# A four-layer decoder on one core: the second layer's attention and projection bias moved into matrix products, and the feed-forward's sums one block later

## The reference

```python
x = x + _L0_ffn_ref(_layernorm(x), router_w, router_b, expert_w, expert_b)   # one of 8 experts for each token
x = x + _L1_attn_ref(_layernorm(x), Wqkv, bqkv, Wproj, bproj)
x = x + _L1_xattn_ref(...)
x = x + _L1_ffn_ref(_layernorm(x), w_gate, w_up, w_down)
```

## Time and profile before

| what | value |
|---|---|
| median of 3 runs | 6096.39 us (6095.18 to 6096.58) |
| the profiled execution | 6100.48 us, of it the span 6098.6 us |
| TensorE busy | 5427.2 us, 89% of the span, granted clock 0.936 in the mean |
| VectorE busy | 3993.1 us, 65% |
| ScalarE busy | 2848.8 us, 47% |
| GpSimd busy | 1761.1 us, 29% |
| loads and stores | 125.10 MB |
| second layer's attention, first product to last output | 1713.89 to 1793.46 us |
| its projection, first turn to the last product | 1793.71 to 1814.58 us |
| second layer's feed-forward, first up to last down product | 2061.05 to 2144.16 us |

### The profile page before, as it was taken

One profiled execution on the slowest core, in us unless ns is written; L12 is line 12 of the kernel. 1 busy time (PEld: TensorE's weight loads), 2 busy tenths in 40 slices (PEclk: granted clock), 3 DMA queues, 4 the chain that ended last, 5 costly groups with the idle time before them and its releaser, 6 DMA issues.

```text
span 6098.6 us, 76361 instructions
## 1 busy us (share of the span) xinstructions
PE 5427.2 (89%) x29994; PEld 2957.3 (48%) x29994; DVE 3993.1 (65%) x6951; ACT 2848.8 (47%) x4524; POOL 1761.1 (29%) x1903
## 2 busy tenths in 40 slices
PE   7987999999977879999998989997958879799978
PEld 4443454454444645555555653336834444333355
DVE  5666767767676579888886257763267744788632
ACT  4553444444115466656564236672135555366600
POOL 3211333333024036454464022203422122222021
PEclk9997999999989989998999889998979989899989
DMA  1000000000000000000000000004410000000033
GB/s 53 1 3 1 1 1 1 1 1 1 21 30 1 8 28 1 1 1 1 1 1 1 10 1 1 1 1 155 166 35 1 1 17 1 32 1 1 32 101 106
DMA packets 39364, 125.10 MB, mean 21 GB/s; under 512 B 5588, under 2 KB 20940, under 8 KB 32990
## 3 DMA queue, kind: packets, MB, share of 16 engines
q1 hardware_dynamic: 28206, 67.70, 3.2%
q0 software_dynamic: 10800, 52.52, 2.5%
HBM read 99.42 MB, written 24.90 MB: 20 GB/s over the span
## 4 chain that ended last, share of the span: by engine, by line


## 5 line engine op out<-in xcount | busy, mean ns | idle before, releaser
L74 PE MATMUL PS<-SC 128*128 128x128 f32 (+14 forms) x14896 | 2814.3, 428 | 163.7 <-ACT SC L80 56.1
L80 ACT ACTIVATE SC<-PS 128x1024 f32<-128x1024 f32 (+7 forms) x2555 | 1933.7, 782 | 1892.6 <-PE PS L74 1560.7
L74 PEld LDWEIGHTS PS<-SC 128*128 128x128 f32 (+6 forms) x14896 | 1214.4, 129 | 1502.6 <-issue 603.7
L95 DVE TENSOR_REDUCE SC<-PS 128x1 f32<-128x512 f32 (+5 forms) x2368 | 1516.6, 680 | 603.0 <-PE PS L74 590.2
L83 POOL TENSOR_TENSOR SC<-SC 128x1024 f32<-128x1024 f32 (+3 forms) x892 | 1190.0, 1344 | 1490.0 <-ACT SC L80 1245.7
L74 PE MATMUL PS<-AR 128*128 128x128 bf16 (+6 forms) x4000 | 1121.6, 393 | 64.2 <-DVE SC L83 16.2
L74 PEld LDWEIGHTS PS<-AR 128*128 128x128 f32 (+2 forms) x4000 | 599.5, 174 | 461.3 <-issue 269.5
L77 PE MATMUL PS<-AR,SC 128*104 128x128 bf16 (+3 forms) x4664 | 518.4, 254 | 322.4 <-DVE SC L86 156.3
L74 PE MATMUL PS<-SC,AR 128*128 128x512 f32 (+7 forms) x1938 | 760.4, 516 | 46.1 <-POOL SC L83 12.8
L77 PEld LDWEIGHTS PS<-AR,SC 128*104 128x104 bf16 (+3 forms) x4664 | 402.1, 135 | 537.6 <-DVE SC L86 142.3
L80 ACT ACTIVATE SC<-SC 128x512 f32<-128x512 f32 (+7 forms) x870 | 445.1, 563 | 454.0 <-DVE SC L86 217.0
(11 more groups left out here) (82 smaller groups left out, 2165.3 us busy)
## 6 DMA issues: line engine op xcount, KB each, us to landing
SC<-in_pk11e SPq DMA_DIRECT2D x8, 1152.0 KB, 5.9
SC<-in_pk11e SPq DMA_DIRECT2D x8, 1028.0 KB, 5.1
xg<-SC SPq DMA_DIRECT2D x16, 512.0 KB, 6.8
SC<-yg SPq DMA_DIRECT2D x16, 512.0 KB, 7.6
yg<-AR SPq DMA_DIRECT2D x8, 512.0 KB, 5.8
AR<-in_pk SPq DMA_DIRECT2D x2, 1562.0 KB, 8.0
AR<-in_pk SPq DMA_DIRECT2D x2, 1538.0 KB, 12.9
AR<-in_pk SPq DMA_DIRECT2D x6, 512.0 KB, 4.9
```

Source lines behind the costliest of these rows:

```text
L74: return Step(self.real and self.real.matmul(*a, **k))
L80: return Step(self.real and self.real.activation(*a, **k))
L95: return Step(self.real and self.real.tensor_reduce(*a, **k))
```

## The change

1. **Bias of the attention as a product.** A new class `Parts` holds the bias row of 1024 values split into three bf16 parts, in partitions 0, 32 and 64 of a tile `bias` that is zero elsewhere, and a bf16 tile of ones, `oneb`. TensorE adds `oneb[0:65].T @ bias[0:65]` to each of the attention's banks (four products a tile) as the last of the accumulation, and to the projection's (`Project` gets an argument `bias`; one product for each of 16 tiles). `AddBias` of stage 3 goes.
2. **Where the parts are made.** The load of `pk3r` moves from stage 3 to the `sp` of `TopOne`, behind `pk2e`; VectorE makes the parts in three pieces after the token tiles i = 1, 2 and 4 of `TopOne`.
3. **PSUM read by ScalarE.** The four reads of a tile's banks are now copies on ScalarE (`out(i)`), with no addition; ScalarE's order is out(0), out(1), exp(0), out(2), exp(1) and so on. `out(i)` waits for the value products of tile i - 2 on VectorE and GpSimd. TensorE waits for ScalarE's copies in place of VectorE's additions.
4. **Feed-forward.** VectorE's loop calls `summed(k - 2)` at f = 1 and `root(k - 2)` at f = 3 of block k, and the sums of blocks 2 and 3 come behind the loop.

```diff
 class Project(Stage):
-                                     start=c == 0, stop=c == 1)
+                                     start=c == 0, stop=c == 1 and self.bias is None)
+                    if self.bias is not None:
+                        t = e.matmul(K.PS[:, 4 + 2 * (k % 2) + g, 256 * z:256 * z + 256], *self.bias, start=False, stop=True)
...
 class TopOne(Stage):
         e.dma_start(self.eb, self.K.ins["pk2e"]).then_inc(self.eb_ready, "all")
+        self.K.parts.sp(e)
...
+            if i in (1, 2, 4):
+                K.parts.dve(e, (1, 2, 4).index(i))
...
+class Parts:
+    def __init__(self, K):
+        heap = Heap(K.view, TOT - 3200, TOT)
+        self.K, self.ready = K, K.load("d_pk3r")
+        self.rows, self.rest = heap.take([1024]), heap.take([1024])
+        self.bias, self.part, self.oneb = heap.take([1024], BF16), heap.take([1024], BF16), heap.take([128], BF16)
+
+    def sp(self, e):
+        e.dma_start(self.rows, self.K.ins["pk3r"]).then_inc(self.ready, "all")
+
+    def dve(self, e, step):
+        vv, bias, part, rest, rows = self.K.vv, self.bias, self.part, self.rest, self.rows
+        if step == 0:
+            e.memset(self.oneb, 1.0).then_inc(vv, "3 one")
+            e.memset(bias, 0.0).then_inc(vv, "3 zero")
+            e.wait_ge(self.ready, "all")
+            e.tensor_copy(part[0:65, :], rows[0:65, :]).then_inc(vv, ("3 part", 0))
+            e.wait_ge(vv, "3 zero")
+            e.tensor_copy(bias[0:1, :], rows[0:1, :]).then_inc(vv, ("3 bias", 0))
+        elif step == 1:
+            e.wait_ge(vv, ("3 part", 0))
+            e.tensor_tensor(rest[0:65, :], rows[0:65, :], part[0:65, :], ALU.subtract).then_inc(vv, ("3 rest", 0))
+            e.wait_ge(vv, ("3 rest", 0))
+            e.tensor_copy(part[0:65, :], rest[0:65, :]).then_inc(vv, ("3 part", 1))
+        else:
+            e.tensor_copy(bias[32:33, :], rest[32:33, :]).then_inc(vv, ("3 bias", 1))
+            e.wait_ge(vv, ("3 part", 1))
+            e.tensor_tensor(rest[64:65, :], rest[64:65, :], part[64:65, :], ALU.subtract).then_inc(vv, ("3 rest", 1))
+            e.wait_ge(vv, ("3 rest", 1))
+            e.tensor_copy(bias[64:65, :], rest[64:65, :]).then_inc(vv, ("3 bias", 2))
...
 class BatchAttention(Stage):   # pe
-                        e.wait_ge(K.vv, ("3 qkv", i - 2, b, z))
+                        e.wait_ge(K.av, ("3 qkv", i - 2, b, z))
...
+                    e.wait_ge(K.vv, ("3 bias", 2))
+                    e.matmul(PS[:, bank, 0:hi - lo], self.oneb[0:65, :], self.bias[0:65, lo:hi], start=False, stop=True).then_inc(K.mm, ("3 qkv", i, b, z))
...
+        def out(i):            # act
+            x = i % 2
+            if i >= 2:
+                e.wait_ge(K.vv, ("3 pv", i - 2, 1))
+                e.wait_ge(K.gv, ("3 pv", i - 2, 1))
+            for b in range(2):
+                for z in range(2):
+                    lo, hi = (0, 512) if z == 0 else (512, 768)
+                    e.wait_ge(K.mm, ("3 qkv", i, b, z))
+                    e.activation(self.qk[x][:, b, lo:hi], K.PS[:, 4 * x + 2 * b + z, 0:hi - lo], ACT.Copy).then_inc(K.av, ("3 qkv", i, b, z))
+        out(0)
         for i in range(8):
-            e.wait_ge(self.K.vv, ("3 s-max", i))
+            if i + 1 < 8:
+                out(i + 1)
+            e.wait_ge(K.vv, ("3 s-max", i))
...
-            for b in range(2):  # dve
-                for z in range(2):
-                    lo, hi = (0, 512) if z == 0 else (512, 768)
-                    e.wait_ge(K.mm, ("3 qkv", i, b, z))
-                    e.tensor_tensor(qk[:, b, lo:hi], PS[:, 4 * x + 2 * b + z, 0:hi - lo], self.rows[:, lo:hi], ALU.add).then_inc(vv, ("3 qkv", i, b, z))
...
-    return [norm, Meet(K, "n3"), AddBias(K, "bias3", K.X, st.rows[:, 768:1024], st.rows_ready), st,
-            Meet(K, "a3"), K.tail]
+    return [norm, Meet(K, "n3"), st, Meet(K, "a3"), K.tail]
...
 class Swiglu(Stage):           # dve
-            if k > 0 and f == 3:
-                summed(k - 1)
-                if self.next is not None:
-                    self.next.root(e, 0, k - 1)
+            if k > 1 and f == 1:
+                summed(k - 2)
+            if k > 1 and f == 3 and self.next is not None:
+                self.next.root(e, 0, k - 2)
         low(4 * nf - 1)
         if self.next is not None:
-            for k in range(3):
+            for k in range(2):
                 self.next.scale(e, 0, k)
-        summed(3)
-        if self.next is not None:
-            self.next.root(e, 0, 3)
-            self.next.scale(e, 0, 3)
+        for k in (2, 3):
+            summed(k)
+            if self.next is not None:
+                self.next.root(e, 0, k)
+                self.next.scale(e, 0, k)
```

More of the change, by code:

```diff
@@ L422, with __init__ @@
     next = None
-    def __init__(self, K, tag, O, wo, dst):
-        self.K, self.tag, self.O, self.wo, self.dst = K, tag, O, wo, dst
+    def __init__(self, K, tag, O, wo, dst, bias=None):
+        self.K, self.tag, self.O, self.wo, self.dst, self.bias = K, tag, O, wo, dst, bias
         self.done = (K.mm, (tag, "o", 3, 1))
@@ L1340, in __init__ @@
         self.norm = EarlyLogits(K, "n2", [layer(K.X, take([NT, D]))], self)
+        K.parts = Parts(K)
     def bank(self, n):
@@ L1507, in __init__ @@
         take = K.scr.take
-        self.rows = take([1024])
-        self.rows_ready = K.load("d_pk3r")
+        self.bias, self.oneb = K.parts.bias, K.parts.oneb
         self.qk = [take([2, 768]) for _ in range(2)]
@@ L1515, in __init__ @@
         self.O = take([NT, D])
-    def sp(self, e):
-        e.dma_start(self.rows, self.K.ins["pk3r"]).then_inc(self.rows_ready, "all")
     def pe(self, e):
@@ L1528, in pe @@
                     if i >= 2:
-                        e.wait_ge(K.vv, ("3 qkv", i - 2, b, z))
+                        e.wait_ge(K.av, ("3 qkv", i - 2, b, z))
                     for c in range(2):
-                        t = e.matmul(PS[:, bank, 0:hi - lo], K.XNT[:, c, b * S + 128 * i:b * S + 128 * i + 128], self.wqkv[:, c, lo:hi],
-                                     start=c == 0, stop=c == 1)
-                    t.then_inc(K.mm, ("3 qkv", i, b, z))
+                        e.matmul(PS[:, bank, 0:hi - lo], K.XNT[:, c, b * S + 128 * i:b * S + 128 * i + 128], self.wqkv[:, c, lo:hi],
+                                 start=c == 0, stop=False)
+                    e.wait_ge(K.vv, ("3 bias", 2))
+                    e.matmul(PS[:, bank, 0:hi - lo], self.oneb[0:65, :], self.bias[0:65, lo:hi], start=False, stop=True).then_inc(K.mm, ("3 qkv", i, b, z))
     def act(self, e):
+        K = self.K
+        def out(i):
[9 more added lines that the diff above has]
+        out(0)
         for i in range(8):
-            e.wait_ge(self.K.vv, ("3 s-max", i))
-            e.activation(self.ex[i % 2], self.sc[i % 2], ACT.Exp, scale=0.25).then_inc(self.K.av, ("3 exp", i))
+            if i + 1 < 8:
+                out(i + 1)
+            e.wait_ge(K.vv, ("3 s-max", i))
+            e.activation(self.ex[i % 2], self.sc[i % 2], ACT.Exp, scale=0.25).then_inc(K.av, ("3 exp", i))
     def dve(self, e):
-        K, PS, vv = self.K, self.K.PS, self.K.vv
-        e.wait_ge(self.rows_ready, "all")
+        K, vv = self.K, self.K.vv
         for i in range(8):
@@ L1547, in dve @@
                 e.wait_ge(K.gv, ("3 pv", i - 2, 1))
-            for b in range(2):
-                for z in range(2):
-                    lo, hi = (0, 512) if z == 0 else (512, 768)
-                    e.wait_ge(K.mm, ("3 qkv", i, b, z))
-                    e.tensor_tensor(qk[:, b, lo:hi], PS[:, 4 * x + 2 * b + z, 0:hi - lo], self.rows[:, lo:hi], ALU.add).then_inc(vv, ("3 qkv", i, b, z))
             Q, Kk, V = qk[:, :, 0:256], qk[:, :, 256:512], qk[:, :, 512:768]
-            e.wait_ge(vv, ("3 qkv", i, 1, 1))
+            e.wait_ge(K.av, ("3 qkv", i, 1, 1))
             for r in range(2):
@@ L1591, in stages_3 @@
     norm = follow(K, Norm(K, "n3", [layer(K.X, st.O)]))
-    K.tail = Project(K, "o3", st.O, st.wo, K.X)
-    return [norm, Meet(K, "n3"), AddBias(K, "bias3", K.X, st.rows[:, 768:1024], st.rows_ready), st,
-            Meet(K, "a3"), K.tail]
+    K.tail = Project(K, "o3", st.O, st.wo, K.X, (st.oneb[0:65, :], st.bias[0:65, 768:1024]))
+    return [norm, Meet(K, "n3"), st, Meet(K, "a3"), K.tail]
 class Row(Stage):
```

## The result

The changed kernel took 6054.65 us (median of 4 runs, 6045.15 to 6062.02) against 6096.49 us for the kernel before on the same chip (6095.18 to 6102.40): ratio 0.9928, 95% interval 0.9916 to 0.9941. Timed again on another chip it took 6058.55 against 6100.10, ratio 0.9931 [0.9917, 0.9944]. The profiled execution took 6057.24 us, its span 6055.2 at a granted clock of 0.941 (before 0.936).

A forecast was written before the change was run, and what follows sets the result against it. VectorE was taken to bound the attention, and TensorE, stopping for VectorE, the feed-forward. Gains of 15.5 and 14.7 us less 1.1 in the projection make 29.1, so 6096.4 becomes 6067.3 us; range 6062 to 6078.

The forecast's parts named there:

- Attention: Second layer's attention: VectorE loses 1.97 us of additions per tile, period 8.65 to 6.68 us; gain 15.5 us.
- The lower price of the bf16 products: Attention, TensorE: a tile's four added products cost 0.71 to 1.32 us; 0.71 was taken.
- Rivals 1 and 5: Bf16 products break TensorE's stream or weight loads stand open, 6075, chance 0.08; array drains around each, 6115, chance 0.03.
- the paragraph on ScalarE's queue: Attention: exp(i) stands behind tile i+1's copies; no cost in steady state, VectorE waits at the start, first exp done at 1727.8.
- Projection: Sixteen added bf16 products; eight ahead of VectorE's wait-free sums cost 1.1 us, the other eight end just as VectorE comes.
- The parts: Expert stage: VectorE's added work making the bias parts, 7.8 us at most in three pieces, costs nothing.
- rival 4: Expert stage: making the bias parts is not hidden, up to 7.8 us, total 6075; chance 0.04.
- Feed-forward: Reordering VectorE's sums removes TensorE's pauses, 11.2 us, and stretches partly at 1.2 GHz; gain 14.7 us.
- Rivals 2 and 3: Feed-forward: sum and statistics stall TensorE again, 6073, chance 0.09; or the new order brings nothing, 6082, chance 0.04.
- The sum: Whole kernel: 15.5 - 1.1 + 14.7 = 29.1 us gained, from 6096.4 to 6067.3 us.
- What follows: Behind the feed-forward: the turn of the sums and the next stage's load move with the last down product.
- a gain beyond forecast: Whole kernel: the case of a gain larger than forecast; chance 0.02.

The follow-up runs named there:

- after_poolbias: Changed kernel with the projection's bias given back to GpSimd and its sixteen products left out; median 6053.31 us.
- before_pause8: Kernel before with a 9.5 us pause of eight VectorE memsets and a meeting of all engines ahead of the second layer's attention; median 6107.95 us.
- ffn_only: Kernel before with only the feed-forward's new VectorE order; median 6076.69 us, ratio 0.9960.

## Why the prediction was right in its stages and wrong in its total

- **Attention, right.** 15.6 us against 15.5: period 6.67 (6.68), tile 5.83 (5.95), first exp at 1726.69 (about 1727.5), no pause of TensorE before the eighth tile, and no slower tile. The lower price of the bf16 products was the right one: 2 x 0.22 + 2 x 0.11 = 0.66 us a tile (0.71). Rivals 1 and 5, dear products and drains, are gone with it: the weight loads of the bf16 products are within the 0.22 and 0.11 us. VectorE waits 4.26 us for the first exp, as the paragraph on ScalarE's queue had it.
- **Projection, near in size and wrong in mechanism.** 1.75 us lost against 1.1, and that they are close is luck: of the 1.1 for products ahead of VectorE's stream 0.26 showed. The larger part is how the next stage's fills on GpSimd meet VectorE's norm, which the working did not have: it names no work of the next stage there. The Trainium skill (SBUF — State Buffer, Who interferes with whom) says that a tensor_scalar can take the pair of ports that VectorE shares with GpSimd, and that the engine which comes second waits for the other's whole instruction. The 2.94 us in place of 0.37 could be such a wait, but not by that rule alone: a fill takes 10.21 / 16 = 0.64 us, and the wait is four times that. What is shown is that the time hangs on where the fills begin: 0.14 or 0.15 us ahead of the last sums the 128x4 takes 0.37 us (before, after_poolbias), 0.16 behind them 2.40 (before_pause8, with no such product in it), 0.74 behind them 2.94 (after). No run took the fills away, so the ports as the cause are argued, not shown.
- **The parts, right.** 6.4 us of VectorE, hidden: rival 4 is gone. after_poolbias tells that the bias of the projection wasn't worth its products, by 1.8 us.
- **Feed-forward, right.** 15.0 us against 14.7; no pause, no sum that waits. Rivals 2 and 3 are gone. ffn_only shows the same 75.9 us with the rest of the kernel as before.
- **The sum, wrong.** The step that failed is the one that ends the sum at the touched stages: "What follows ... is released by the same last down product and moves with it". It does move, but it does not keep its length: 14.0 of the 43.4 us by which the span fell lie outside the touched stages, 8.6 of them behind the Mamba stage and 5.3 in it. TensorE is busy for 89% of the span and is granted 1.2 GHz for stretches of it, and how long differs between profiles, of one and the same program too. The sum put this at nothing without a reason, and gave a gain beyond forecast a chance of 0.02. The term that was missing is the untouched stages' own spread: 5886.9 to 5905.7 us outside in seven profiles of the kernel before, pauses or none, and 5882.7 to 5896.6 in nine of the changed one and its near versions. That is 19 and 14 us from end to end, as wide as the whole range of 6062 to 6078, which carried only bounds of the diff's own costs. The first three runs' 6095.18 to 6096.58 hid it: in later runs the kernel before took 6088.7 to 6109.8.
- **What stays open.** About 8 of the 12.6 us go when both kernels are shifted, 1 of them in the touched stages themselves. The last 4 to 5 (33.3 against 28.9) are no more than these medians can be off; the mean time outside, 5895.4 in the seven profiles and 5887.9 in the nine, leans the same way, and so do the 5 us behind the Mamba stage. What decides the length of a stretch at the lower clock, the start of the stage, something the new attention leaves behind, or the chance of the execution, isn't settled.

## What to carry to other kernels

Where an order of work leaves an engine idle for another's latest product, asking for the product one block later is free and worth the whole pause (15.0 us here). The sum over the touched stages came out 0.2 us off from rows alone (29.1 against 28.9), with terms that were off by 0.1, 0.65 and 0.3 and partly made up for each other. The total can't be had so: ahead of a forecast, compare stages between repeats of the same kernel, and give the range at least that spread. To judge a change of some 0.5%, shift both kernels by a small pause or two and compare the distances too; they still scatter by 2 us here, and a pause has a price of its own.

## What was not expected of the hardware

- The same stage of the same program took 1292.0 and 1302.4 us, at equal work on all other engines and with TensorE at 20.00 of 20.00 us busy where the clock was 0.66.
- Behind a pause of 1.5 us the Mamba stretch took 4.9 us less in the kernel before and 4.4 more in the changed one (1286.55 to 1290.92); behind one of 3.5 us it had its old length within 0.15 us in all three kernels. Without a pause it took 1291.91 and 1281.51, and 1286.55 and 1280.55, in two profiles each, so no single step of this is sure to be the pause's work.
- A 128x4 operation of VectorE took 2.94 us with GpSimd's memsets beside it; at 1797.14, ahead of them, the same one took 0.17. In the kernel before, memsets beside it too, it took 0.37, and 2.40 with a pause ahead, so it is the moment that decides.
